# Order of operations on TensorE and ScalarE in the edge loops of a four-layer graph network

## The reference

```python
h_s, h_v = lin1(s), lin1(v)                        # node tables
w = silu(edge_scalars @ fc_w1) @ fc_w2             # weights of each edge
w1, w2, w3, w4, w5 = split(w, [64, 128, 160, 192])
es, ev = h_s[edge_src], h_v[edge_src]              # gathered rows
m_s1 = w1 * es * e0
m_s2 = w4 * einsum('eci,ei->ec', ev, e1)
m_v1 = (w2 * es)[:, :, None] * e1[:, None, :]
m_v2 = w3[:, :, None] * ev * e0[:, :, None]
m_v3 = w5[:, :, None] * cross(ev, e1)
agg_s, agg_v = segment_sum(...), segment_sum(...)  # over the edge's node
x = layernorm(x + gated(lin2(agg) + skip(x)))
```

## Time and profile before

| what | us |
|---|---|
| median of 3 runs | 10883.89 |
| lowest and highest run | 10879.81, 10886.22 |
| the profiled execution | 10889.87 |
| its span in the profile | 10887.1 |
| edge loop of layer 1, first to last L1041 | 5756.5 to 7258.5 |
| edge loop of layer 2, first to last L1041 | 7567.9 to 9017.4 |
| edge loop of layer 3, first to last L1041 | 9195.7 to 10698.6 |

### The profile page before, as it was taken

How to read it: one execution, slowest core, us unless ns; L and a number is a source line. 1 busy time by engine, 2 the same in 40 slices (tenths; PEclk the granted TensorE clock), 3 DMA queues, 4 the chain that set the end, 5 groups by cost and what they waited for, 6 DMA issues and landing times. The chain is left out here.

```text
span 10887.1 us, 242413 instructions
## 1 busy us (share of the span) xinstructions
PE 8864.7 (81%) x46500; PEld 6212.8 (57%) x46501; DVE 8658.5 (80%) x31135; ACT 6961.3 (64%) x26255; POOL 6465.1 (59%) x9502
## 2 busy tenths in 40 slices
PE   3570069999999999999997888887888887888887
PEld 1250058888888888888884444445444445444445
DVE  6850069999999999999978999974666666999995
ACT  0020058888888888888875666644777775777774
POOL 0577777777777777777525555531555551555551
PEclk9965589999999999999999999985999998999996
DMA  7433322222222212221123444441333333444443
GB/s 292 44 82 73 71 42 37 36 37 36 37 36 37 36 35 37 36 36 34 20 43 84 90 89 89 89 67 36 58 58 58 58 57 66 90 90 90 90 89 58
DMA packets 1798441, 691.91 MB, mean 64 GB/s; under 512 B 1586190, under 2 KB 1677258, under 8 KB 1798346
## 3 DMA queue, kind: packets, MB, share of 16 engines
q0 software_dynamic: 219136, 411.56, 15.6%
q1 hardware_dynamic: 1572154, 275.26, 15.1%
q10 hardware_dynamic: 7056, 4.02, 0.1%
HBM read 514.24 MB, written 171.77 MB: 63 GB/s over the span
## 5 line engine op out<-in xcount | busy, mean ns | idle before, releaser
L911 POOL DMA_INDIRECT shared<-table,rec x2640 | 2564.6, 971 | 2236.0 <-DMA efr<-rec_dst 786.9
L993 PE MATMUL bank<-tp,oh 128*128 128x480 f32 (+1 forms) x5280 | 2352.4, 541 | 7.2 <-DVE tp L1070 4.2
L945 ACT ACTIVATE tp<-tp,rec 128x64 f32<-128x64 f32 x7920 | 2031.2, 335 | 239.3 <-DVE tp L1041 174.8
L985 PE MATMUL bank<-w_fc,hT 128*128 128x448 f32 x2640 | 1346.2, 592 | 589.2 <-ACT hT L929 573.0
L993 PEld LDWEIGHTS bank<-tp,oh 128*128 128x128 f32 x5280 | 902.0, 191 | 831.9 <-issue 819.4
L782 POOL DMA_INDIRECT rec_dst<-ACC x784 | 811.6, 1035 | 529.7 <-issue 497.3
L1041 DVE TENSOR_TENSOR tp<-bank,shared 128x256 f32<-128x256 f32 x1320 | 560.6, 425 | 653.9 <-PE bank L993 516.6
L1630 ACT ACTIVATE shared<-bank 128x512 f32<-128x512 f32 x1760 | 942.9, 586 | 122.1 <-PE bank L1705 119.3
L1594 POOL DMA_INDIRECT gat<-table,rec x880 | 889.5, 1011 | 220.5 <-issue 202.6
L929 ACT ACTIVATE hT<-bank 128x128 f32<-128x128 f32 x1320 | 366.5, 278 | 989.2 <-PE bank L979 964.3
L1581 POOL DMA_INDIRECT rec_src<-ACC x784 | 841.6, 1074 | 208.0 <-issue 185.4
(11 more groups left out here) (249 smaller groups left out, 21496.4 us busy)
## 6 DMA issues: line engine op xcount, KB each, us to landing
shared<-table,rec POOLq DMA_INDIRECT x2640
rec_dst<-tp SPq DMA_DIRECT2D x44, 900.0 KB, 23.6
ACC<-in_attrs SPq DMA_DIRECT2D x56, 623.0 KB, 5.1
rec_src<-tp SPq DMA_DIRECT2D x44, 730.0 KB, 19.8
efr<-rec_src SPq DMA_DIRECT2D x440, 64.0 KB
efr<-rec_dst SPq DMA_DIRECT2D x440, 64.0 KB
ACC<-in_attrs SPq DMA_DIRECT2D x196, 130.0 KB
rec<-rec_dst SPq DMA_DIRECT2D x1320, 10.0 KB
```

The costliest lines, as they stand in the source:

```text
L911: nc.gpsimd.indirect_dma_start(out=gatx[:, u, g, 0:L.row], out_offset=None, in_=tables[L.n][:, :], in_offset=IOff(ap=rec[:, u, g, L.idx:L. ...
L945: done = nc.scalar.activation(t[:, g, lo:lo + 64], t[:, g, 0:64], ACT.Copy, scale=rec[:, u, g, L.y + k:L.y + k + 1])
L985: nc.tensor.matmul(pW[u % 2][:, 0:448], hT[:, u % 2, :], fc2[:, :], start=True, stop=True)\
L993: done = nc.tensor.matmul(pS[u % 2][:, 0:TW], oh[:, u, g, :], tp[:, u % 2, g, 64:64 + TW], start=g == 0, stop=g == G - 1)
```

## The change

TensorE's step of the edge loop issues the first matmul of `sums` ahead of `weights`. ScalarE's step issues `features` ahead of `scaled`. What each computes, its waits and its buffers stay. The parts ahead of the loops, which fill the pipeline, are unchanged. The loop of layer 0 is not touched.

```diff
                     def step(i, u, end=False):
                         axes(i, u)
+                        if not end or last(u, 2):
+                            features(*after(i, u, 2))
                         if L.y0 is not None and (not end or last(u, 1)):
                             scaled(*after(i, u, 1))
                         if not end or last(u, 2):
-                            features(*after(i, u, 2))
                             activated(*after(i, u, 2))
...
                     def step(i, u, end=False):
+                        sums(i, u, 0)
                         if not end or last(u, 2):
                             weights(*after(i, u, 2))
-                        sums(i, u, 0)
                         if not end or last(u, 3):
                             transposed(*after(i, u, 3))
                         sums(i, u, 1)
```

## The result

| us | before | after |
|---|---|---|
| median of 4 runs each | 10882.53 | 10614.32 |
| lowest and highest | 10879.81, 10886.22 | 10611.76, 10616.28 |
| ratio, with its 95% interval | | 0.9749 [0.9738, 0.9761] |
| span of the profile | 10887.1 | 10610.0 |
| loop of layer 1, first to last product | 1501.9 | 1456.6 |

The forecast was 10634 with 10540 to 10730. The three loops lose 45.3 + 182.6 + 49.4 = 277.3 us, which is the whole difference of the spans (277.1). The medians of the runs differ by 268 us: the profiled execution before was 7 us longer than the median, the one after 3 us shorter. From line 998 on, the lines of the kernel after are one higher: the product is L1042, the sums are L994, the weights L986.

What follows compares the result with a forecast made beforehand. No engine was full; a cycle of waits between TensorE and ScalarE set the pace. Gains of 111 (layers 1 and 3) and 181 (layer 2), less 42 for gathers, give 250: 10884 - 250 = 10634 us, range 10540 to 10730.

Steps and rivals of the forecast that it cites:

- The cycle over hT: Edge loops: TensorE's weights wait 0.44 us a step for ScalarE's activated (hT); layer 2's closed chain is 3.27 us.
- Layers 1 and 3, 3.27 from VectorE: With the first sum ahead of the weights, VectorE just bounds layers 1 and 3 at 3.27 us a step, gaining 111 us.
- the sum of the forecast: VectorE in layer 1: three steps of 3.18 us and one of 3.54 at its loop turn, 13.08 in all.
- 111 - 22 = 89 us: Layers 1 and 3 together: 111 us gained by shorter steps, less 11 us a layer for late gathers.
- that rival, 10723: VectorE already bounds layers 1 and 3, so only layer 2 gains, 181 - 20: 10723 us; chance 0.14.
- Layer 2, 2.84 from ScalarE's cycle: Layer 2, product to product over axes, copy and scalings: 2.79 plus 0.05 for loop turns, 2.84 us a step; gains 181 us.
- The sign that was asked for: In layer 2 VectorE's product (L1041) waits for ScalarE's L935 in place of the sums at L993.
- its mis-sized term: ScalarE's copy in layer 2's cycle, put at 0.24 to 0.30 us and taken as its own length, 0.27.
- TensorE's step was put at 2.44 to 2.82: Layer 2: TensorE's two sums, weights, transpose and hidden matmul take 2.44 to 2.82 us, not above 2.84.
- 181 - 20 = 161 us: Layer 2: 181 us gained by shorter steps, less 20 us for late gathers (12 steps x 1.7).
- Gathers, 42 us: Shorter steps take slack from gathers, so VectorE waits more: 11 us each in layers 1 and 3, 20 in layer 2.
- Last 24 steps unchanged: The last 24 or so steps of each loop are another regime and stay at 3.65 us.
- Slower, by late scaled weights: ScalarE's copy waits for the transpose, delaying scaled and VectorE's product; layer 3 at 3.50 us, total 10921 us; chance 0.03.

Runs made afterwards that it cites:

- r1_after: The kernel after, unedited, run on chip B beside the kernel before: 11422.42 us against 11382.53, ratio 1.0033.
- e2_scalar_only: The kernel before with ScalarE's part of the change alone (features ahead of scaled), on chip A: 11292.47 us, ratio 1.0003.

## Why the prediction was right

**The cycle over hT** was the pace, and it opened: 573.0 to 3.1 us of waiting at the weights. Right.

**Layers 1 and 3, 3.27 from VectorE.** The medians of the four steps of a turn are 3.184, 3.181, 3.175 and 3.536 in layer 1, together 13.08, the sum of the forecast. With gathers the step is 3.295 and 3.293; 111 - 22 = 89 us were forecast, 94.7 measured. The mechanism is right: VectorE is idle only at loop turns and late gathers now, and with less work its step gets shorter. The Trainium skill, Perfetto Trace Analysis, section Identifying the Most-Contended Engine, says to optimize the engine of highest occupancy first. The prediction took from it a rival by which a reordering on TensorE gives nothing in these layers, and that rival, 10723, fell. Occupancy as a measure of what is left agrees with the traces: VectorE was 95% busy, and its step fell by 3.2%.

**Layer 2, 2.84 from ScalarE's cycle.** 2.842 measured, but the agreement is partly luck, for the cycle that was forecast is not what paces the loop. The sign that was asked for came: L1042 waits for L935 in 343 of some 370 steps. It does not tell the two cycles apart: `scaled` comes last for VectorE in either case, and ScalarE itself is idle before `activated` in every step while TensorE never rests. ScalarE's cycle was put at 2.79 and is 2.70 in the step shown. The copy is its mis-sized term: 0.27 was added for it, its own length, while the scalings start 0.15 after it (8402.33 to 8402.48). TensorE's step was put at 2.44 to 2.82 and called no bound; it is 2.77, with its loop's turn 2.81, and is the bound. Its low end is also a wrong sum: with the 0.10 that it names the terms add up to 2.54. `hidden` had been put at 0.20 to 0.48 and takes 0.41. So the right number came from a cycle priced some 0.1 too long, beside one whose price had been left wide and whose loop turn had been left out.

181 - 20 = 161 us were forecast and 182.6 measured. The medians of the four steps of a turn are 2.692, 2.824, 2.768 and 2.947, a mean of 2.808: 13 us better than 2.84 over 416 steps. The mean step is (2.842 - 2.808) x 407 = 14 us above that, mostly late gathers, for which 20 had been set, and the last 24 steps gave 2 that were not forecast.

**Gathers, 42 us.** From the whole run, waits of the first product operation for gathers before, then after:

```profile
DVE tp L1041 <- DMA shared<-table,rec: 61.2, 70, 2.9
```

```profile
DVE tp L1042 <- DMA shared<-table,rec: 105.2, 112, 2.4
```

44.0 us more, in 42 more steps. The total held, its shares did not: in the steps 9 to 416 the wait grew from 6 to 10 us in layer 1, from 0 to 37 in layer 2 and from 6 to 10 in layer 3, where 11, 20 and 11 were forecast. In layer 2 it costs less than it shows, since VectorE would have waited there for `scaled` anyway.

**Last 24 steps unchanged.** 3.66 in layer 1, 3.59 in layers 2 and 3 where 3.66 was: 3 us more gained. Right in substance, and the cause is the padding's gathers.

**Slower, by late scaled weights.** On the first chip it did not come. On the four others the change, or TensorE's part of it alone, is 0.3 to 0.6% slower, yet not by this mechanism, which would have made layer 3 slower than layer 1: in `r1_after` they take 3.59 and 3.64 us a step. What goes with the loss are the stalls: on chip A the time above the fast steps grew by 241 us where the fast steps saved 212. The forecast had no such case at all, and that is the largest thing it missed: all its terms came from one undisturbed trace.

## What to carry over

When no engine is full, look for the closed chain of waits, add its links from the timeline, and ask what is late next on every engine once it opens; here that gave three step times within 1%, one of them through the wrong cycle. When two cycles stand within the width of their prices, the wait at the end of one doesn't tell which leads: look for the engine that never idles. Moving a copy ahead of longer work on the same engine is worth nothing until the engine that waits for it is early enough: each half must be costed with the other in place. A gain that consists of tighter waits between engines holds only where releases arrive on time: measure it on more than one chip before counting on it. Where stalls cover a comparison, the fast quarter of the steps, place by place in the loop's turn, can still show it.

## What was not expected of the hardware

- The same program took 10880 to 10886 us on one chip and 11250 to 11442 on four others, with the durations of computing instructions alike (the product's first operation 425 ns in layer 1 in the kernel before on the first chip and in `e2_scalar_only`). The traces of the four show stalls, which lengthen single steps by up to 5 us; releases arrive late in them and SyncE's register instructions last up to 1.5 us. Their cause is open.
- After a stall that left TensorE idle for 3.60 us its granted clock was 0.50 for some 10 us. The loop of layer 2 spent 155 us so in `e2_scalar_only` and 324 us in `r1_after`, whose steps are shorter.
- Gathers whose descriptors all read one row hold the DMA engines about twice as long as gathers of different rows at the same GB/s (0.65 against 0.27 in layer 2).
